# A state-space scan carried as h plus A·u: ScalarE divides u by the decay rate into PSUM, VectorE adds neighbouring tokens of two groups at once, decays in SBUF

## The chip, the core and the metric

One core of one Trainium2 chip runs the kernel. The time is device microseconds from the start to the end of one execution; the runs shown are medians of 3. The core has a matrix engine (TensorE, PE), VectorE (DVE), ScalarE (ACT), GpSimd (POOL), and a sync engine (SyncE, SP) that here only issues DMAs. Each takes its instructions strictly in order, and they meet at semaphores.

## What is computed

Four images of 3x224x224 go through a token stage (two small attention blocks over 3x3 patches, then a projection), which gives 3136 tokens of 768 channels per image. Then comes a selective state-space layer and a layer of experts. The state-space layer is what the change touches:

```
delta = softplus(x @ W_D + b_D + p_Delta)         # per token and channel
A_bar = exp(delta * A)                            # A = -1..-16, one per state n
B_bar = (A_bar - A) / (delta * A) * delta * Bproj # = (A_bar - A) / A * Bproj
h     = A_bar * h + B_bar * x                     # recurrence over tokens
y     = sum_n C_n * h_n
```

With u = B·x the input of one state is (A_bar − A)·u/A. There are 768 channels x 16 states = 12288 independent recurrences, each 3136 tokens long, per image.

## The kernel before

The program has three stages, one after the other: `performer1`, `performer2` and `tail` (line 1298). Only `tail` is touched, and it takes more than half of the time.

`tail` cuts the tokens into UNITS = 28 units (4 images x 7) of T = 448 tokens. In each unit the recurrences are done in STEPS = 24 steps, so 672 in all: step k = Q·dc + q (Q = 4) handles channel chunk dc of six (128 channels) and four of the 16 states. The 128 partitions of a step hold 32 channels x 4 states, and the free axis holds 4 groups g of 32 channels with 448 tokens each. A row of the ring `v` (RING = 6 steps deep) has 4 groups of GW = 452 columns. Step n goes through the engines like this:

- GpSimd, `weigh_in` (L1615, instruction at L1624): v = x·B, all four groups in one instruction of 128x1792. `weigh_out` (L1627, at L1636) multiplies the scanned states by C, 128x1792 again. GpSimd's order is in(k), out(k−2).
- ScalarE, `step` (L1926, at L1935): the decay exp(A·delta), one instruction per group, from `dr` in SBUF into PSUM banks 0 to 3 (`decay`, L1311), which hold one step only; so `free_pair` (L1909) makes it wait for the scan of the step before on the same pair of groups. `start_states` (L1898, at L1906) puts the last state of the unit before in front of the rows, `keep_states` (L1890, at L1896) saves the last state of a step; `weigh_out` waits for it.
- VectorE, `weigh` (L2045, at L2052): (decay − A)·v, one scalar_tensor_tensor per group; `scan` (L2054, at L2061): one tensor_tensor_scan over the 901 columns of a pair of groups. Per step that is, twice: two `weigh`, one `scan`.
- TensorE, `step` (L1725, at L1736): sums the states with `dg`, a table of diagonal matrices that carry 1/A, into bank YB; after four steps it adds h itself (L1740), and ScalarE copies the sum back into h (`add_to_h`, L1920, at L1924).

Between the steps each engine does the rest of the unit before and of the unit after. Their places are written out by hand, in the table at L1443 to L1453: a number is the step k after which an engine does the work, and on ScalarE k + 0.5 is the slot after the second pair of a step.

```
A_HW, A_SQ, A_MU, A_RS = (4, 6.5, 8, 9.5, 10.5, 12), (9.5, 12.5), 15.5, 15.5
A_MX, A_SP = (17.5, 17.5), ((18, 18.5), (19, 19.5))
V_BC, V_DL = 15, (18, 19)
A_SQ2, A_MS, A_RS2, A_EX, A_OH, A_GL = (1, 5.5), 7.5, 9.5, 12, 14, 17
V_ENC, V_IN, V_LOG, V_EQ, V_MASK = 9, (12, 14, 16, 16), 10, 11, (17, 17, 19, 19)
```

What the prediction speaks of: P_PJ is the projection of a channel chunk on TensorE (L1672, L1674) and A_HW ScalarE's copy of it into h (L1859). A_GL is four Gelu instructions (L1964) between two loads of the function table (the second from L1965). A_MX (L1880), A_SP (L1885 and L1888) and V_DL (L2042) make delta; V_BC (L2033 to L2036) makes B and C; V_IN (L2101) and V_MASK (L2127) belong to the experts; A_EX (L1956) is a small exponential for which VectorE's V_EQ waits. SyncE writes h, delta, B and C to DRAM and reads them back spread over the partitions (`spread_x`, `spread_delta`, `spread_b`, `spread_c`).

Of the kernel before, what the change touches and what calls it, by code (L numbers as in the profile page):

```python
# [21 lines left out]
T = 448  # L22
# [1256 lines left out]
RING = 6  # L1279
GW = T + 4  # L1280
AR, YB, BS, BX, BF = 4, 4, 5, 6, 7
OWN = ()
FEW = NX + 1
CAP = 30.0

def others(n):

    i, k = divmod(n, STEPS)
    return i * (STEPS - len(OWN)) + sum(j not in OWN for j in range(k + 1))  # L1290

def owned(n):

    return n + 1 - others(n)

def tail(nc, sem, w, c, t2, w1c, xd, dd, bcd, out):

    with ExitStack() as ctx:  # L1300
# [10 lines left out]
        def decay(g):  # L1311

            at = g // 2 * 1024 + g % 2 * GW
            return flat[:, at + 2:at + T + 2]

        def decays(pair):
            row = flat[:, 1024 * pair:1024 * pair + 2 * GW]
            return row.rearrange("p (g t) -> p g t", g=2)[:, :, 2:T + 2]
# [26 lines left out]
        dg = sb("dg3", [128, 4 * STEPS, 32])  # L1345
# [7 lines left out]
        mu = sb("mu", [128, 2, T])  # L1353
# [5 lines left out]
        st = sb("st3", [128, 4 * STEPS])  # L1359
        ex = sb("ex", [CH, NCH, NX])  # L1360
# [6 lines left out]
        ai, sel32, encb, wm = gm[:, 0, 0:4 * STEPS], gm[:, 1, 0:32], gm[:, 2, 0:CH], gm[:, 3, 0:6]  # L1367
# [11 lines left out]
        br, cr, zr = slice(0, N), slice(32, 32 + N), slice(32, 33 + N)  # L1379
        low, mid, top = slice(0, 32), slice(32, 64), slice(96, 128)  # L1380
# [4 lines left out]
                 (wbc[:, :, :], w["wbc"]), (pick[:, :, :], c["pick"]), (bbc[:, :], w["bbc"]), (pd[:, :], w["pd"]),  # L1385
# [9 lines left out]
        s_dgm = sem("t_diagonals_made")  # L1395
# [53 lines left out]
        P_PJ, P_SUM, P_Z = (1, 3, 4, 5, 7, 8), (9, 11), 15  # L1449
        A_HW, A_SQ, A_MU, A_RS = (4, 6.5, 8, 9.5, 10.5, 12), (9.5, 12.5), 15.5, 15.5  # L1450
        A_MX, A_SP = (17.5, 17.5), ((18, 18.5), (19, 19.5))
        V_BC, V_DL = 15, (18, 19)
        P_SUM2, P_VAR, P_IN, P_LOG, P_TURN = (2, 4), 6, (10, 11, 13, 14), 8, 10  # L1453
        P_MASK, P_OUT = (15, 15, 16, 17), (18, 19, 20, 20, 21, 22, 23, 24)
        A_SQ2, A_MS, A_RS2, A_EX, A_OH, A_GL = (1, 5.5), 7.5, 9.5, 12, 14, 17
        A_OUT = (22, 22.5, 23.5, 24, 25, 26, 27, 28)
        V_ENC, V_IN, V_LOG, V_EQ, V_MASK = 9, (12, 14, 16, 16), 10, 11, (17, 17, 19, 19)
        ROUTE, TAIL = 9, 29

        def means(i):  # L1460

            return mu[few, i % 3, :] if i % 3 < 2 else bcs[few, :]
# [16 lines left out]
        def _(sp):  # L1479
# [65 lines left out]
            def spread_c(i, q):  # L1545
                if i < UNITS:
                    for own in (True, False):
                        k = max((k for k in range(q, STEPS, Q) if (k in OWN) == own), default=None)
                        if i >= 1 and k is not None:
                            n = STEPS * (i - 1) + k  # L1550
                            sp.wait_ge(s_cv if own else s_cm, 2 * owned(n) if own else others(n))
                    spread_row(ct[:, q, :], i, 1, q).then_inc(s_lc[q], 16)
# [3 lines left out]
            sp.wait_ge(s_set, 9)  # L1556
# [14 lines left out]
            for i in range(UNITS):  # L1571
                for k in range(STEPS):
# [39 lines left out]
        def _(pool):  # L1612
            tt = nc.gpsimd.tensor_tensor

            def weigh_in(i, k):  # L1615
# [8 lines left out]
                tt(v[:, n % RING, :, 2:T + 2], xr[:, dc % 2, :].rearrange("p (i t) -> p i t", i=4), bt[:, q:q + 1, :].to_broadcast([128, 4, T]),  # L1624
                   ALU.mult).then_inc(s_v, 1)

            def weigh_out(i, k):  # L1627

                dc, q = divmod(k, Q)
                if dc == 0:  # L1630
                    pool.wait_ge(s_lc[q], 16 * (i + 1))
                if k in OWN:
                    return
                n = STEPS * i + k
                pool.wait_ge(s_st, others(n))
                tt(v[:, n % RING, :, 2:T + 2], v[:, n % RING, :, 2:T + 2], ct[:, q:q + 1, :].to_broadcast([128, 4, T]),  # L1636
                   ALU.mult).then_inc(s_cm, 1)
# [7 lines left out]
            pool.memset(v[:, :, :, T + 2:GW], 0.0).then_inc(s_set, 1)  # L1645
            pool.memset(v[:, :, :, 0:1], 0.0).then_inc(s_set, 1)
            pool.wait_ge(s_w, 16 * len(loads))
            pool.wait_ge(s_pd, 1)
            tt(dg[:, :, :], sel32[:, :].unsqueeze(1).to_broadcast([128, 4 * STEPS, 32]),
               ai[:, :].unsqueeze(2).to_broadcast([128, 4 * STEPS, 32]), ALU.mult).then_inc(s_dgm, 1)  # L1650
            for i in range(UNITS):
                for k in range(STEPS):
                    weigh_in(i, k)
                    if k >= 2:
                        weigh_out(i, k - 2)
                    elif i >= 1:
                        weigh_out(i - 1, STEPS - 2 + k)
            for k in range(STEPS - 2, STEPS):
                weigh_out(UNITS - 1, k)

        @block.tensor
        def _(pe):
# [32 lines left out]
            def front(i, k):  # L1695
                for dc in range(DC):
# [22 lines left out]
                if k == P_Z:  # L1719
# [3 lines left out]
                    mm(bank(BF), pick[mid, 0, :], bcs[mid, :], start=True, stop=True).then_inc(s_z, 1)  # L1723

            def step(i, k):  # L1725
# [5 lines left out]
                if k in OWN:  # L1731
                    pe.wait_ge(s_cv, 2 * owned(n))
                else:
                    pe.wait_ge(s_cm, others(n))
                for g in range(4):
                    last = mm(ps[32 * g:32 * g + 32, YB, 0:T], dg[:, 4 * k + g, :], v[:, n % RING, g, 2:T + 2],  # L1736
                              start=(q == 0), stop=False)
                last.then_inc(s_ns, 1)
                if q == Q - 1:
                    mm(bank(YB), ident[:, :], h[:, i % 3, dc, :], start=False, stop=True).then_inc(s_hs, 1)  # L1740

            def mlp(i, k):
# [9 lines left out]
                for m in range(MT):  # L1752
# [10 lines left out]
                    if m == 3:  # L1763
                        pe.wait_ge(s_bcs, 2 * min(i + 3, UNITS))
# [55 lines left out]
            pe.wait_ge(s_bcs, 2)  # L1820
# [4 lines left out]
            pe.wait_ge(s_dgm, 1)  # L1825
# [13 lines left out]
        def _(act):  # L1839
# [50 lines left out]
            def keep_states(i, k):  # L1890

                n = STEPS * i + k
                if k in OWN:
                    return
                act.wait_ge(s_sc, 2 * others(n))
                fn(st[:, 4 * k:4 * k + 4], v[:, n % RING, :, T + 1], ACT.Copy).then_inc(s_st, 1)  # L1896

            def start_states(i, k):  # L1898

                n = STEPS * i + k  # L1900
                if k in OWN:
                    return
                after(act, s_ns, n + 1 - RING)
                if i >= 1:
                    act.wait_ge(s_st, others(n - STEPS))
                fn(v[:, n % RING, :, 1], st[:, 4 * k:4 * k + 4], ACT.Copy,  # L1906
                   scale=0.0 if i % J3 == 0 else 1.0).then_inc(s_s0, 1)

            def free_pair(n, pair):  # L1909

                i, k = divmod(n, STEPS)
                if k in OWN:
                    act.wait_ge(s_cv, 2 * owned(n) + pair - 1)
                    at = 4 * k + 2 * pair
                    fn(st[:, at:at + 2], decays(pair)[:, :, T - 1], ACT.Copy).then_inc(s_sv, 1)
                    act.wait_ge(s_sv, 2 * owned(n) + pair - 1)
                else:
                    act.wait_ge(s_sc, 2 * others(n) + pair - 1)
# [6 lines left out]

            def step(i, k, pair):  # L1926

                dc, q = divmod(k, Q)
                n = STEPS * i + k
                if q == 0 and pair == 0:  # L1930
                    act.wait_ge(s_dr[dc % 2], 16 * ((DC // 2) * i + dc // 2 + 1))
                if n > 0:
                    free_pair(n - 1, pair)
                for g in range(2 * pair, 2 * pair + 2):
                    fn(decay(g), dr[:, dc % 2, g, :], ACT.Exp,  # L1935
                       scale=aa[:, 4 * k + g:4 * k + g + 1]).then_inc(s_a, 1)
# [56 lines left out]
            act.wait_ge(s_set, 9)  # L1993
            act.preload_act_table_set(BOTH)
            for k in range(2 * STEPS):
                front(0, k / 2)
            for i in range(UNITS + 1):
                for k in range(TAIL if i == UNITS else STEPS):
                    if i < UNITS:
                        start_states(i, k)  # L2000
                        step(i, k, 0)
# [5 lines left out]
                    if i >= 1 and k == 0:  # L2007
                        keep_states(i - 1, STEPS - 1)
                    elif i < UNITS and k > 0:
                        keep_states(i, k - 1)  # L2010
                    if i < UNITS:
                        step(i, k, 1)
# [5 lines left out]
        def _(dve):  # L2018
# [8 lines left out]
            def front(i, k):  # L2027
                if k == V_BC:
# [7 lines left out]
                    stt(bcs[br, :], ps[br, BS, 0:T], bbc[br, :], rs1[br, :], ALU.add, ALU.mult).then_inc(s_bcs, 1)  # L2036
                for half in range(2):
# [293 lines left out]
```

## Time and profile before

| | us |
|---|---|
| median of 3 runs | 8061.27 (8054.65 to 8067.14) |
| the profiled execution: its own time | 8056.0 |
| its span, first to last instruction | 8054.2 |
| busy in the span: PE, DVE, ACT, POOL | 7205.3, 6156.8, 4377.1, 5546.6 |
| mean granted TensorE clock | 0.927 of full speed |

The first two stages end at about 3200 us; the rest is `tail`. A share of busy time over the whole span mixes the stages, so the rows that matter are read within `tail`. An instruction's duration is longer than the distance between the starts of two that follow each other directly, as an engine begins the next one before the last has drained; both are used below, and told apart.

### The profile page before, as it was taken

The page shows a single profiled execution, that of the slowest core. Times are in us where ns is not written, and L with a number is a line of the kernel's source. Part 1 is how long each engine was busy: PE and PEld are TensorE (multiplying, and loading weights), DVE is VectorE, ACT ScalarE, POOL GpSimd, SP SyncE. Part 2 cuts the span into 40 slices and gives each one's busy share as a digit, 9 for nine tenths or more (in the row PEclk, how much of TensorE's full clock was granted, in tenths as well). Part 3 has the DMA queues.
Part 4 walks back from the last instruction along what each step waited for, and adds up shares of the span by engine and source line. Part 5 has one row for each costly group of instructions (what it writes and reads, how often), then busy time and mean ns, then how long its engine had stood idle before and what let it go on. Part 6 is the DMA issues. An engine that isn't in the chain of part 4 may idle for free.

```text
span 8054.2 us, 87036 instructions
## 1 busy us (share of the span) xinstructions
PE 7205.3 (89%) x31060; PEld 2876.3 (36%) x31060; DVE 6156.8 (76%) x6517; ACT 4377.1 (54%) x7837; POOL 5546.6 (69%) x2487
## 2 busy tenths in 40 slices
PE   8999999979999995689889898898888988988888
PEld 6444444323443431133333333333333333333323
DVE  2566666761333333999999999999999999999995
ACT  3566666763344442555555555555555555555553
POOL 0011111128766640999999999999999999999994
PEclk9999999989999997799899999899998999989988
DMA  1111111125545423333333333333334333334331
GB/s 40 33 46 45 42 44 43 42 60 114 105 98 109 100 61 84 101 116 113 131 130 125 112 119 125 126 124 126 119 109 136 122 128 113 117 128 132 125 110 56
DMA packets 358649, 786.32 MB, mean 98 GB/s; under 512 B 72229, under 2 KB 284727, under 8 KB 350729
## 3 DMA queue, kind: packets, MB, share of 16 engines
q1 hardware_dynamic: 320838, 689.44, 29.1%
q0 software_dynamic: 21712, 51.75, 2.5%
q10 hardware_dynamic: 15666, 39.57, 1.4%
q8 instruction: 246, 4.03, 0.2%
q14 instruction: 187, 1.52, 0.1%
HBM read 597.06 MB, written 183.35 MB: 97 GB/s over the span
## 4 chain that ended last, share of the span: by engine, by line
DVE 34%; issue 13%; ACT 7%; PE 6%; POOL 1%; DMA 0%; DVEq 0%; SPq 0%; ACTq 0%
DVE v L2052 16%; DVE v L2061 15%; ACT ps L1935 2%; PE ps L1672 2%; DVE dl L2042 1%; PE ps L1674 1%; PE ps L1667 1%; ACT dl L1880 1%; ACT gm L1964 1%; PE ps L1802 1%; PE ps L1681 1%; PE ps L1736 1%; ACT dl L1885 0%; ACT L1965 0%; ACT L1964 0%
## 5 line engine op out<-in xcount | busy, mean ns | idle before, releaser
L2061 DVE TENSOR_TENSOR_SCAN v<-ps,v 128x901 f32<-128x901 f32 x1344 | 2732.3, 2033 | 93.4 <-DVE v L2052 0.9
L1636 POOL TENSOR_TENSOR v<-v,ct 128x1792 f32<-128x1792 f32 x672 | 2258.2, 3360 | 288.8 <-ACT st L1896 285.6
L1624 POOL TENSOR_TENSOR v<-xr,bt 128x1792 f32<-128x1792 f32 x672 | 2258.2, 3361 | 65.8 <-DMA bt<-bc_rows 65.8
L1935 ACT ACTIVATE ps<-dr,aa 128x448 f32<-128x448 f32 x2688 | 1596.0, 626 | 1087.4 <-DVE v L2061 1077.7
L2052 DVE SCALAR_TENSOR_TENSOR v<-ps,aa,v 128x448 f32<-128x448 f32 x2688 | 1686.2, 669 | 11.5 <-ACT ps L1935 5.4
L236 POOL DMA_DIRECT2D tokens<-ob x448 | 235.3, 532 | 1533.5 <-DVE ob L563 1490.5
L1736 PE MATMUL ps<-v,dg 128*32 128x448 f32 x5376 | 779.3, 617 | 476.9 <-POOL v L1636 251.8
L1802 PE MATMUL ps<-w_or_w,gm 128*112 128x384 f32 x1792 | 692.4, 534 | 67.8 <-DVE gm L2127 65.0
L1896 ACT ACTIVATE st<-v 128x4 f32<-128x4 f32 x672 | 140.7, 209 | 912.5 <-DVE v L2061 910.6
L1672 PE MATMUL ps<-x,wpa 128*128 128x448 f32 x1008 | 479.0, 613 | 85.9 <-ACT h L1859 75.1
L1667 PE MATMUL ps<-h,w_or_w 128*128 128x448 f32 x1344 | 538.3, 551 | 9.7 <-DVE bcs L2036 9.7
L1802 PEld LDWEIGHTS ps<-w_or_w,gm 128*112 128x112 f32 x1792 | 331.3, 193 | 439.8 <-issue 121.6
L1674 PE MATMUL ps<-x,wpb 64*128 64x448 f32 x1008 | 450.5, 578 | 0.0
L1736 PEld LDWEIGHTS ps<-v,dg 128*32 128x32 f32 x5376 | 136.1, 113 | 856.7 <-POOL v L1636 375.1
L929 PE MATMUL ps<-xt,wa 128*64 128x448 f32 x2016 | 435.0, 565 | 0.0
L552 DVE COPY ht<-ps 112x512 f32<-112x512 f32 x112 | 77.4, 691 | 466.6 <-ACT kp L433 466.6
L1667 PEld LDWEIGHTS ps<-h,w_or_w 128*128 128x128 f32 x1344 | 251.4, 192 | 294.0 <-issue 264.5
L1238 DVE TENSOR_TENSOR kq<-ps,rsa 128x896 f32<-128x896 f32 x56 | 61.1, 1092 | 358.7 <-PE ps L937 337.5
L586 DVE RECIPROCAL qpn<-qpn 128x448 f32<-128x448 f32 x112 | 330.7, 2953 | 3.8
L1672 PEld LDWEIGHTS ps<-x,wpa 128*128 128x128 f32 x1008 | 190.9, 201 | 338.8 <-issue 230.5
L290 PE MATMUL ps<-wki,h 128*112 128x256 f32 x896 | 277.3, 391 | 1.9 <-DVE hu L544 1.9
L1674 PEld LDWEIGHTS ps<-x,wpb 64*128 64x128 f32 x1008 | 174.7, 186 | 271.0 <-issue 271.0
(331 smaller groups left out, 11534.1 us busy)
## 6 DMA issues: line engine op xcount, KB each, us to landing
xr<-h_by_channel SPq DMA_DIRECT2D x168, 896.0 KB, 5.0
dr<-delta_by_channel SPq DMA_DIRECT2D x168, 896.0 KB, 4.7
x<-tokens SPq DMA_DIRECT2D x252, 224.0 KB, 5.3
tokens<-ob POOLq DMA_DIRECT2D x448, 112.0 KB, 2.4
w_or_w<-in_w SPq DMA_DIRECT2D x29, 1536.0 KB, 6.4
w_or_w<-centred_w SPq DMA_DIRECT2D x27, 1536.0 KB, 9.1
h_by_channel<-h SPq DMA_DIRECT2D x112, 336.0 KB, 5.1
delta_by_channel<-dl SPq DMA_DIRECT2D x224, 168.0 KB, 2.8
```

Of the source, the lines that this page charges most:

```text
L586: nc.vector.reciprocal(qpn[:, u % 3, :], qpn[:, u % 3, :]).then_inc(s_dr, 1)
L929: mm(ps[half[g], o, 0:T], wa[:, j, cols], xt[:, 2 * (n % 3) + g, 0:TR2, j:j + 2 * S2 - 1:2], start=(j == 0), stop=False)
L1624: tt(v[:, n % RING, :, 2:T + 2], xr[:, dc % 2, :].rearrange("p (i t) -> p i t", i=4), bt[:, q:q + 1, :].to_broadcast([128, 4, T]), ALU.mul ...
L1636: tt(v[:, n % RING, :, 2:T + 2], v[:, n % RING, :, 2:T + 2], ct[:, q:q + 1, :].to_broadcast([128, 4, T]), ALU.mult).then_inc(s_cm, 1)
L1667: last = mm(into, weights(dc), h[:, i % 3, dc, :], start=(dc == 0), stop=(dc == DC - 1))
L1672: mm(into, even(j), x3[:, 0:TR3, j:j + 2 * S3 - 1:2], start=(j == 0), stop=False)
L1674: return mm(into, odd(j - 3), x3[0:64, 1:TR3 + 1, j - 3:j - 4 + 2 * S3:2], start=False, stop=(j == 5))
L1736: last = mm(ps[32 * g:32 * g + 32, YB, 0:T], dg[:, 4 * k + g, :], v[:, n % RING, g, 2:T + 2], start=(q == 0), stop=False)
L1802: mm(into[:, 0:D // 2], gm[:, m, cs], w2[:, m, lo:lo + D // 2], start=(m == 0), stop=False)
L1935: fn(decay(g), dr[:, dc % 2, g, :], ACT.Exp, scale=aa[:, 4 * k + g:4 * k + g + 1]).then_inc(s_a, 1)
L2052: stt(row, decay(g), aa[:, 4 * k + g:4 * k + g + 1], row, ALU.subtract, ALU.mult).then_inc(s_wt, 1)
L2061: nc.vector.tensor_tensor_scan(row, flat[:, 1024 * pair + 1:1024 * pair + GW + T + 2], row, 0.0, ALU.mult, ALU.add).then_inc(s_sc, 1)
```

## The change

Before, a row holds A·h, and one VectorE pass per group forms (decay − A)·u. Written for s = −(h + u), the recurrence is s(t) = decay(t)·(s(t−1) + u(t−1) − u(t)/A): what enters the scan is −u/A of the token plus u of its left neighbour, and the scan adds first and multiplies then. (In the units of before that state is A·h plus A·u.) Since h = −s − u, the sum over states leaves out the direct part, x times the sum of B·C over the states; it is taken off h once per unit. In the code:

- ScalarE, `divide` (new): one copy per group with the scale 1/A (negative, from `ai`), from `v` in SBUF into PSUM banks 0 to 3, 449 columns. `decays` (new): the exponentials go into a new SBUF buffer `da`, two steps deep, one step ahead of `divide`. Order of a step: start_states(n+1), divide(n, pair 0), decays(n+1, pair 0), the other work, keep_states(n−1), divide(n, pair 1), decays(n+1, pair 1), the other work.
- VectorE, `differences` (new) in place of two `weigh`: one tensor_tensor add over both groups of a pair, 128x898, in place in PSUM; `scan` reads PSUM and `da`, adds, then multiplies, over 901 columns as before. New per unit: C·B (one scalar_tensor_tensor of 16x448 in V_BC) and, at V_HK = 23, h·(1 − sum of B·C), one scalar_tensor_tensor of 128x2688.
- TensorE: `dg` is gone; the sum uses one matrix `sel32` of −1. One new matmul per unit (P_KP = 19) spreads B·C.
- GpSimd: `weigh_out` runs BEHIND = 3 steps behind `weigh_in` instead of 2; the making of `dg` is gone, two small memsets are new.
- SyncE: one more small constant is loaded; load_x moves from k = 13 to 16, the load of w2 from 15 to 16.
- The table of places is written anew.

```
-            def weigh(i, k, g):
...
-                dve.wait_ge(s_a, 4 * n + g // 2 * 2 + 2)
-                row = v[:, n % RING, g, 2:T + 2]
-                stt(row, decay(g), aa[:, 4 * k + g:4 * k + g + 1], row, ALU.subtract, ALU.mult).then_inc(s_wt, 1)
...
+            def differences(n, pair):
+
                 if pair == 0:
-                    dve.wait_ge(s_s0, others(n))
-                dve.wait_ge(s_wt, 4 * n + 2 * pair + 2)
-                nc.vector.tensor_tensor_scan(row, flat[:, 1024 * pair + 1:1024 * pair + GW + T + 2], row, 0.0, ALU.mult,
-                                             ALU.add).then_inc(s_sc, 1)
+                    dve.wait_ge(s_s0, n + 1)
+                dve.wait_ge(s_ux, 4 * n + 2 * pair + 2)
+                tt(quotients(pair), quotients(pair), v[:, n % RING, 2 * pair:2 * pair + 2, 2:T + 3],
+                   ALU.add).then_inc(s_wt, 1)
+
+            def scan(n, pair):
...
+                dve.wait_ge(s_wt, 2 * n + pair + 1)
+                dve.wait_ge(s_a, 4 * n + 2 * pair + 2)
+                nc.vector.tensor_tensor_scan(row[:, 2:GW + T + 3], flat[:, 1024 * pair + 2:1024 * pair + GW + T + 3],
+                                             a[:, 2:GW + T + 3], 0.0, ALU.add, ALU.mult).then_inc(s_sc, 1)
...
+            def decays(n, pair):
+
+                dc, q = divmod(n % STEPS, Q)
+                if q == 0:
+                    act.wait_ge(s_dr[dc % 2], 16 * ((DC // 2) * (n // STEPS) + dc // 2 + 1))
+                after(act, s_sc, 2 * n + pair - 3)
+                for g in range(2 * pair, 2 * pair + 2):
+                    at = 4 * (n % STEPS) + g
+                    fn(da[:, n % 2, g, 2:T + 2], dr[:, dc % 2, g, :], ACT.Exp, scale=aa[:, at:at + 1]).then_inc(s_a, 1)
+
+            def divide(n, pair):
+
+                act.wait_ge(s_v, n + 1)
+                after(act, s_sc, 2 * n + pair - 1)
+                for g in range(2 * pair, 2 * pair + 2):
+                    at = 4 * (n % STEPS) + g
+                    fn(quotient(g), v[:, n % RING, g, 3:T + 4], ACT.Copy, scale=ai[:, at:at + 1]).then_inc(s_ux, 1)
...
+                    dve.wait_ge(s_bcs, 2 * (i + 1))
+                    after(dve, s_kp, i)
+                    stt(cc, ps[cr, BS, 0:T], bcc[br, :], bcs[br, :], ALU.add, ALU.mult).then_inc(s_cb, 1)
+                if k == V_HK:
+                    dve.wait_ge(s_kp, i + 1)
+                    dve.wait_ge(s_xst, 64 * (i + 1))
+                    stt(h[:, i % 3, :, :], ps[:, BF:BF + 1, 0:T].to_broadcast([128, DC, T]), 1.0, h[:, i % 3, :, :],
+                        ALU.add, ALU.mult).then_inc(s_hk, 1)
...
-        P_PJ, P_SUM, P_Z = (1, 3, 4, 5, 7, 8), (9, 11), 15
-        A_HW, A_SQ, A_MU, A_RS = (4, 6.5, 8, 9.5, 10.5, 12), (9.5, 12.5), 15.5, 15.5
-        A_MX, A_SP = (17.5, 17.5), ((18, 18.5), (19, 19.5))
-        V_BC, V_DL = 15, (18, 19)
-        P_SUM2, P_VAR, P_IN, P_LOG, P_TURN = (2, 4), 6, (10, 11, 13, 14), 8, 10
-        P_MASK, P_OUT = (15, 15, 16, 17), (18, 19, 20, 20, 21, 22, 23, 24)
-        A_SQ2, A_MS, A_RS2, A_EX, A_OH, A_GL = (1, 5.5), 7.5, 9.5, 12, 14, 17
-        A_OUT = (22, 22.5, 23.5, 24, 25, 26, 27, 28)
-        V_ENC, V_IN, V_LOG, V_EQ, V_MASK = 9, (12, 14, 16, 16), 10, 11, (17, 17, 19, 19)
+        P_PJ, P_SUM, P_Z = (0, 3, 5, 6, 7, 8), (8, 11), 15
+        A_HW, A_SQ, A_MU, A_RS = (4, 7.5, 8, 9.5, 10.5, 11.5), (9.5, 12.5), 16, 15.5
+        A_MX, A_SP = (17.5, 18.5), ((18, 18.5), (18.5, 18.5))
+        V_BC, V_DL = 15, (18, 18)
+        P_KP, V_HK = 19, 23
+        P_SUM2, P_VAR, P_IN, P_LOG, P_TURN = (2, 4), 6, (9, 11, 13, 13), 8, 9
+        P_MASK, P_OUT = (15, 15, 16, 16), (17, 18, 19, 20, 21, 22, 23, 24)
+        A_SQ2, A_MS, A_RS2, A_EX, A_OH, A_GL = (0, 5.5), 7.5, 8.5, 12, 14.5, 17
+        A_OUT = (21, 22, 23, 23.5, 24.5, 25.5, 26.5, 27.5)
+        V_ENC, V_IN, V_LOG, V_EQ, V_MASK = 8, (12, 14, 16, 16), 10, 11, (17, 17, 18, 18)
```

## Rows read from the trace of the kernel before

**Rows 1.** The profile page, part 1: busy time, share and instructions of each engine.

```profile
PE 7205.3 (89%) x31060; PEld 2876.3 (36%) x31060; DVE 6156.8 (76%) x6517; ACT 4377.1 (54%) x7837; POOL 5546.6 (69%) x2487
```

**Rows 2.** Busy time of each engine in one stretch of the last stage, granted clock, DMA.

```profile
5000.00:5500.00 500.00, 442.69 (x1630) 162.56 (x1628) 488.42 (x505) 283.70 (x596) 470.99 (x142) 0.91 0.38 125
```

**Rows 3.** VectorE in order of time, five pieces of undisturbed steps: start, us, instruction.

```profile
5075.51 2.03 DVE L2061 TENSOR_TENSOR_SCAN v<-ps,v 128x901 f32<-128x901 f32 x1
5077.46 1.25 DVE L2052 SCALAR_TENSOR_TENSOR v<-ps,aa,v 128x448 f32<-128x448 f32 x2
5078.74 2.03 DVE L2061 TENSOR_TENSOR_SCAN v<-ps,v 128x901 f32<-128x901 f32 x1
5080.69 1.25 DVE L2052 SCALAR_TENSOR_TENSOR v<-ps,aa,v 128x448 f32<-128x448 f32 x2
5082.05 2.03 DVE L2061 TENSOR_TENSOR_SCAN v<-ps,v 128x901 f32<-128x901 f32 x1
```

**Rows 4.** GpSimd: the line of `weigh_in` over the whole trace, and two neighbours in time.

```profile
L1624 POOL TENSOR_TENSOR v<-xr,bt x672: 3347/3359/3392, 3198.6 to 7935.4; 128x1792 f32<-128x1792 f32 x168
...
5061.56 3.36 POOL L1636 TENSOR_TENSOR v<-v,ct 128x1792 f32<-128x1792 f32 x1
5064.88 3.36 POOL L1624 TENSOR_TENSOR v<-xr,bt 128x1792 f32<-128x1792 f32 x1
```

**Rows 5.** Groups by line and shape, VectorE, whole trace: busy us, mean ns, idle before.

```profile
L2061 DVE TENSOR_TENSOR_SCAN v<-ps,v 128x901 f32<-128x901 f32 x1344 | 2732.3, 2033 | 93.4 <-DVE v L2052 0.9 <-ACT v L1906 0.5
L558 DVE TENSOR_TENSOR gl<-ps,rs 128x896 f32<-128x896 f32 x112 | 121.2, 1082 | 6.0 <-PE ps L265 6.0
L1238 DVE TENSOR_TENSOR kq<-ps,rsa 128x896 f32<-128x896 f32 x56 | 61.1, 1092 | 358.7 <-PE ps L937 337.5 <-issue 21.2
L2042 DVE SCALAR_TENSOR_TENSOR dl<-ps,pd,dl 128x448 f32<-128x448 f32 x168 | 103.6, 671 | 8.1 <-ACT dl L1888 8.1
L2143 DVE TENSOR_TENSOR wpa<-wpa,wma 128x2304 f32<-128x2304 f32 x1 | 2.6, 2559 | 0.0
```

**Rows 6.** Groups by line and shape, ScalarE, whole trace.

```profile
L1935 ACT ACTIVATE ps<-dr,aa 128x448 f32<-128x448 f32 x2688 | 1596.0, 626 | 1087.4 <-DVE v L2061 1077.7 <-DMA dr<-delta_by_channel 9.3
L1924 ACT ACTIVATE h<-ps 128x448 f32<-128x448 f32 x168 | 89.1, 530 | 5.3 <-PE ps L1740 5.3
L1964 ACT ACTIVATE gm<-gm,b 128x448 f32<-128x448 f32 x112 | 68.9, 660 | 11.4 <-DVE gm L2101 10.5
```

**Rows 7.** ScalarE in order of time around its steps 17 to 19 of one unit.

```profile
5018.13 1.20 ACT L1935 ACTIVATE ps<-dr,aa 128x448 f32<-128x448 f32 x2 [3.83 <-DVE v L2061]
5019.34 1.28 ACT L1964 ACT_TABLE_LOAD   x1
5020.63 2.47 ACT L1964 ACTIVATE gm<-gm,b 128x448 f32<-128x448 f32 x4
5023.12 1.28 ACT L1965 ACT_TABLE_LOAD   x1
...
5024.53 1.18 ACT L1935 ACTIVATE ps<-dr,aa 128x448 f32<-128x448 f32 x2
5025.73 3.26 ACT L1880 ACTIVATE dl<-ps,pc 128x448 f32<-128x448 f32 x6
...
5030.48 1.45 ACT L1885 ACTIVATE dl<-dl,small 128x1344 f32<-128x1344 f32 x1
...
5033.01 1.34 ACT L1888 ACTIVATE dl<-dl 128x1344 f32<-128x1344 f32 x1
```

**Rows 8.** VectorE in order of time, the experts' work within the same steps.

```profile
5021.24 1.13 DVE L2101 TENSOR_TENSOR gm<-ps,rs2t 128x448 f32<-128x448 f32 x2
...
5029.01 1.12 DVE L2127 TENSOR_TENSOR gm<-gm,ps 128x448 f32<-128x448 f32 x2
```

**Rows 9.** Who waited for whom on ScalarE, 4000 to 7500 us: total us, times, longest.

```profile
ACT ps L1935 <- DVE v L2061: 789.7, 403, 4.7
ACT h L1859 <- PE ps L1674: 34.4, 25, 3.2
```

More of the change, by code:

```diff
@@ L1279 @@
 RING = 6
+BEHIND = 3
 GW = T + 4
 AR, YB, BS, BX, BF = 4, 4, 5, 6, 7
-OWN = ()
 FEW = NX + 1
 CAP = 30.0
[L1287 to L1295, printed above, removed]
 def tail(nc, sem, w, c, t2, w1c, xd, dd, bcd, out):
@@ L1309, in tail, with quotient, quotients @@
         flat = ps[:, :, :].rearrange("p k n -> p (k n)")
-        def decay(g):
+        def quotient(g):
             at = g // 2 * 1024 + g % 2 * GW
-            return flat[:, at + 2:at + T + 2]
-        def decays(pair):
+            return flat[:, at + 2:at + T + 3]
+        def quotients(pair):
             row = flat[:, 1024 * pair:1024 * pair + 2 * GW]
-            return row.rearrange("p (g t) -> p g t", g=2)[:, :, 2:T + 2]
+            return row.rearrange("p (g t) -> p g t", g=2)[:, :, 2:T + 3]
         ident = sb("ident3", [128, 128])
@@ L1546, in spread_c @@
                 if i < UNITS:
[L1547 to L1551, printed above, removed]
+                    after(sp, s_cm, STEPS * (i - 1) + STEPS - Q + q + 1)
                     spread_row(ct[:, q, :], i, 1, q).then_inc(s_lc[q], 16)
@@ L1819, in _ @@
             pe.wait_ge(s_wv, 16)
[L1820 removed]
+            pe.wait_ge(s_cb, 1)
             pe.wait_ge(s_mu, 1)
@@ L1924, in add_to_h @@
                 fn(h[:, i % 3, dc, :], bank(YB), ACT.Copy).then_inc(s_hy, 1)
[L1926 to L1936, printed above, removed]
             def mlp(i, k):
@@ L1996, in _ @@
                 front(0, k / 2)
+            start_states(0)
+            for pair in range(2):
+                decays(0, pair)
             for i in range(UNITS + 1):
                 for k in range(TAIL if i == UNITS else STEPS):
+                    n = STEPS * i + k
+                    if n + 1 < STEPS * UNITS:
+                        start_states(n + 1)
                     if i < UNITS:
-                        start_states(i, k)
-                        step(i, k, 0)
+                        divide(n, 0)
+                    if n + 1 < STEPS * UNITS:
+                        decays(n + 1, 0)
                     if i >= 1 and k == 2:
@@ L2006, in _ @@
                     others_due(i, k)
[L2007 to L2010, printed above, removed]
+                    if 0 < n <= STEPS * UNITS:
+                        keep_states(n - 1)
                     if i < UNITS:
-                        step(i, k, 1)
+                        divide(n, 1)
+                    if n + 1 < STEPS * UNITS:
+                        decays(n + 1, 1)
                     others_due(i, k + 0.5)
@@ L2081, in step @@
             def step(i, k):
                 for pair in range(2):
-                    weigh(i, k, 2 * pair)
-                    weigh(i, k, 2 * pair + 1)
-                    if k in OWN:
-                        own_scan(i, k, pair)
-                    else:
-                        scan(i, k, pair)
+                    differences(STEPS * i + k, pair)
+                    scan(STEPS * i + k, pair)
             def mlp(i, k):
```

144 lines of the change are left out of this document (58 added, 86 removed).

## The prediction

> **What bounds the kernel now.** I read the page's busy shares first, then the windows inside the last stage, then each engine in order of time. Over the whole span TensorE looks busiest [rows 1], but that mixes three stages. In a window of the last stage VectorE is busy 488 of 500 us, GpSimd 471, TensorE 443, ScalarE 284 [rows 2]. In order of time VectorE shows no gap [rows 3], while ScalarE waits 790 us for VectorE's scans in 3500 [rows 9]: VectorE sets the pace.
>
> The sizes: `weigh_in` starts at 3198.6 for step 0 and at 7935.4 for step 671 [rows 4], so a step takes 7.06 us and a unit of 24 steps 169.4. Undisturbed, two pairs of VectorE's take 82.05 − 75.51 = 6.54 us [rows 3], 157.0 a unit; the other 12.4 us are its work for the experts, delta, B and C. GpSimd starts an instruction every 3.32 us [rows 4], 6.64 a step, 159.2 a unit. That is the next floor: whatever VectorE saves, no more than 169.4 − 159.2 = 10.2 us a unit, 286 us in 28 units, can be had.
>
> **VectorE: the difference.** A pair is now: scan, and 1.95 us after its start the first of two `weigh`; from that start to the next scan 1.28 or 1.36 us, as the last one has to land and a semaphore be passed (0.03 us behind the landing with one wait, 0.11 with two) [rows 3]. Mean 3.27. After: one add of 128x898. Two rows have its size and kind, 1082 and 1092 ns for 896 columns [rows 5]; I take 1.085. Its output lies in PSUM, which neither row shows; the ends are 1.08 and, if it cost no less than the two instructions it replaces, 1.25. Both scans now pass two semaphores (differences, decays), so 0.11 twice. 1.95 + 1.085 + 0.11 = 3.145: saved 0.125 x 1344 = **168 us**.
>
> The scan keeps its 901 columns and one PSUM and one SBUF input, but adds before it multiplies. No row shows that form. I take the 2033 ns of [rows 5]; upward nothing in the trace bounds it better than a few per cent (5% would be 137 us), downward one operation in the loop instead of two would halve it, and then GpSimd's floor is met. 
>
> **VectorE: what is added.** h·(1 − sum) over 2688 columns: between 896 and 2304 columns a VectorE column costs (2559 − 1092)/1408 = 1.04 ns [rows 5], so 2.96 us, less about 0.08 of overlap: 2.9. C·B: as the 671 ns row [rows 5] with its wait, 0.7. Together 3.6 x 28 = **101 us**, all of it on the engine that sets the pace. VectorE alone thus gains only 67 us.
>
> **ScalarE: is it still cover?** It now issues eight big instructions a step instead of four. Nearest to the scaled copy are the exponential with a scale from memory, 626 ns, and the plain copy from PSUM, 530 [rows 6]; a pair of the former lasts 1.18, so starts lie 0.56 apart [rows 7]. I take 0.56 for all four of a half step, plus 0.11 for the small state copy: 2.35 of 3.145 us. Today it is 1.23 of 3.27. Its other work is 284/500 x 169.4 = 96 us a unit less 48 x 1.23 = 37 us; new total 48 x 2.35 + 37 = 150 us of some 166. On average it fits; the question is bursts. PSUM still holds one step, so a quotient can't be made ahead: from the end of the scan that frees it, 0.03 + 0.11 + 0.56 + 0.62 = 1.3 us go by until the pair is ready, and VectorE wants it after 3.06. The reserve is 1.75 us, and each half step has only 0.8 us for other work. Decays a step ahead do not widen it, since they stand in the same queue behind the divide.
>
> At k = 17 stand the Gelus with both table loads, 5019.34 to 5024.40 = 5.06 us [rows 7]. Let T be the end of the first scan of step 16. ScalarE: half step to T + 2.35, Gelus to 7.4, quotients of (17, pair 1) ready at 8.7. VectorE, with its two V_IN products of 1.13 [rows 8], wants them at 3.06 + 1.13 + 3.145 = 7.3: stall 1.4. Next, three A_MX (half of 3.26) end at 11.4; VectorE finds (18, 0) ready. h copy and exponential, 0.5 + 1.4, put (18, 1) at 16.95; VectorE, with two V_MASK of 1.12 [rows 8], wants it at 16.1: stall 0.85. The slot 18.5 holds 1.65 + 1.34 + 1.4 + 1.34 = 5.7 us [rows 7] and ends at 23.7; VectorE needs the last logarithm for delta at 23.0: stall 0.7. Sum 2.95 x 27 = **80 us**; ends 0 and 5 us a unit.
>
> Elsewhere ScalarE waits for TensorE's projections, 34.4 us in 20.7 units, at most 3.2 [rows 9], today inside its idle time. In the new table A_HW's last copy (11.5) stands ahead of A_EX (12), for which VectorE waits. Of the 1.7 us a unit I let 0.6 through: **16 us**, ends 0 and 47.
>
> The Trainium skill (ScalarE: Activation LUTs, in the part on the pipeline for one element) prefers PSUM to SBUF as ScalarE's target and so speaks against moving the decays. Here the scaled exponential into PSUM has 626 ns and the Gelu within SBUF 660 [rows 6], which agrees in sign; at 0.034 us more for two instructions the burst stalls would be about 0.3 us a unit longer, 8 us in all.
>
> **What costs nothing.** GpSimd one step further behind: it waits for the state copies, so the in-order product behind it is late, but its 10 us of idle time a unit cover that; without the cover each late product delays TensorE's sum by 3.3 us and `add_to_h` after it. The making of `dg` at the start: GpSimd waits there for B's transfer anyway. TensorE's new matmul, one of about 0.6 us a unit: 443 of 500 busy leaves 19 us a unit. SyncE's loads moved to k = 16: h and weights are used from k = 0 and 17 on, 8 and more steps or the masks' wait later; a weight load late would show as TensorE waiting for a DMA. `dr` is wanted one step (6.6 us) earlier, but is also released one step earlier, and at a unit's turn there remain four steps. At the start the first step waits for four exponentials and two copies instead of two exponentials: **3 us**.
>
> **Sum.** −168 + 101 + 80 + 16 + 3 = +32 us on the profiled execution's 8056.0: 8088. The median of the runs shown is 5 us above it, so 8093 for a median. A measurement tells about 0.2%, 16 us, from no change.
>
> **Rivals.** *ScalarE keeps up* (faster). The two late stalls vanish if the real copies are nearer the plain 530 ns, and work VectorE does meanwhile fills the rest: 8061 − 67 + 3 = 7997, down to 7950 if the semaphore costs 0.03 throughout (−47). For it: 790 us of ScalarE idle [rows 9]. Against: the Gelu block is three times the reserve, and its position is written in the table. It decides where the quotients of step 17, pair 1, come within 7.3 us of T.
>
> *ScalarE becomes the bound.* If scaled copies and exponentials into SBUF come 0.60 apart like the Gelus ((2.47 − 0.66)/3, [rows 7]), a half step has 0.6 us left, each wait for TensorE's projections falls on VectorE whole (1.7 us), the burst stalls grow to about 4.5 and the bursts at 7.5 to 9.5 stall for another 1.5: 7.7 us a unit, 8061 − 67 + 3 + 215 = 8212. For it: 2.35 of 3.145 us are gone before any other work; against it: the averages still leave 10%.
>
> *The replacement doesn't do what it says.* If the add over PSUM takes 1.25 us, a pair lasts 3.31 instead of 3.27 and nothing is saved: 8061 + 54 + 101 + 3 = 8219 before any stall. If the scan were cheaper by half, GpSimd sets the pace at 159.2 a unit: 8061 − 286 = 7775, little changed by anything else.
>
> **Chances.** Forecast (the gain given back by stalls and the new products) 0.47, its own range 8035 to 8140; ScalarE keeps up 0.32; ScalarE the bound 0.16; dearer add or scan 0.03; cheaper scan 0.02. Faster by over 0.2% takes the second case, the last and a little of the first; no change the first's lower part. The range 7960 to 8220 leaves out some 2 in 10.
>
> **What would show it.** VectorE's adds near 1085 ns, 1344 of them, and the scans still at 2033; a pair 3.1 to 3.2 us apart in undisturbed steps; VectorE idle before the add, waiting for ScalarE's copies, 50 to 150 us in all and most of it around the Gelus; ScalarE busy near 90% in the last stage; the product over 2688 columns near 2.96 us. I am wrong if VectorE shows no such waits (then it is faster), if they are spread over all steps (then ScalarE is the bound), or if GpSimd is seen without idle time.

## The result, and the profile after

The changed kernel takes 7980.58 us (median of 4 runs, 7977.03 to 7982.75) against 8062.83 for the kernel before on the same chips: ratio 0.9898, 95% interval 0.9886 to 0.9911. It is 1.0% faster; the forecast was 8093 us, slower by 0.4%. The profiled execution took 7978.7 us, its span is 7977.0, 77.2 us shorter than before. The first step of the last stage starts where it did, so all of it was won in the 672 steps.

Part 1 of the page, as in [rows 1]:

```profile
PE 7204.1 (90%) x31116; PEld 2913.0 (37%) x31116; DVE 6031.6 (76%) x5230; ACT 5851.7 (73%) x10525; POOL 5539.2 (69%) x2488
```

and the window of 5000 to 5500 us, with the columns of [rows 2] (us; busy and count of PE, its weight loads, DVE, ACT, POOL; clock; DMA share; GB/s):

```profile
5000.00:5500.00 500.00, 448.36 (x1668) 170.27 (x1668) 483.23 (x375) 445.00 (x893) 477.62 (x145) 0.94 0.38 124
```

ScalarE went from 284 to 445 of 500 us, 89%, as forecast. VectorE fell from 488 to 483 and GpSimd rose from 471 to 478: no engine is full any more, and four engines lie within 38 us of each other. The groups by line, as in [rows 5] and [rows 6]:

```profile
L2051 DVE TENSOR_TENSOR_SCAN v<-ps,da 128x901 f32<-128x901 f32 x1344 | 2732.5, 2033 | 46.1
L2042 DVE TENSOR_TENSOR ps<-ps,v 128x898 f32<-128x898 f32 x1344 | 1452.3, 1081 | 74.2 <-ACT ps L1907 70.7
L1907 ACT ACTIVATE ps<-v,ai 128x449 f32<-128x449 f32 x2688 | 1593.6, 625 | 222.9 <-DVE v L2051 216.4
L1899 ACT ACTIVATE da<-dr,aa 128x448 f32<-128x448 f32 x2688 | 1634.0, 656 | 9.5 <-DMA dr<-delta_by_channel 9.5
```

The scan kept its 2033 ns, the add costs 1081, the scaled copy 625 and the exponential into SBUF 656 instead of 626 into PSUM: durations as they were priced. What was not priced right is a distance. VectorE in order of time (compare [rows 3]):

```profile
5071.94 2.03 DVE L2051 TENSOR_TENSOR_SCAN v<-ps,da 128x901 f32<-128x901 f32 x1
5073.89 1.07 DVE L2042 TENSOR_TENSOR ps<-ps,v 128x898 f32<-128x898 f32 x1
5075.00 2.03 DVE L2051 TENSOR_TENSOR_SCAN v<-ps,da 128x901 f32<-128x901 f32 x1
5076.95 1.07 DVE L2042 TENSOR_TENSOR ps<-ps,v 128x898 f32<-128x898 f32 x1
5078.06 2.04 DVE L2051 TENSOR_TENSOR_SCAN v<-ps,da 128x901 f32<-128x901 f32 x1
```

A pair takes 3.06 us, not 3.145: behind the end of the add the scan starts after 0.03 us, in both pairs, though it waits for two semaphores. Before, the mean pair took 3.27. That is 0.21 x 1344 = 282 us saved in place of 168.

The burst (the stretch of k = 17 to 18.5 with the Gelus, the two table loads and the work for delta on ScalarE) went as worked out. ScalarE from the half step (17, pair 0) to the last logarithm of delta, with the lines that bound it, and VectorE's three waits in it:

```profile
4990.72 1.20 ACT L1907 ACTIVATE ps<-v,ai 128x449 f32<-128x449 f32 x2 [1.41 <-DVE v L2051]
...
4993.09 1.28 ACT L1941 ACT_TABLE_LOAD   x1
4994.38 2.35 ACT L1941 ACTIVATE gm<-gm,b 128x448 f32<-128x448 f32 x4
4996.75 1.28 ACT L1942 ACT_TABLE_LOAD   x1
...
5012.71 1.32 ACT L1874 ACTIVATE dl<-dl 128x1344 f32<-128x1344 f32 x1
```

```profile
4999.37 1.10 DVE L2042 TENSOR_TENSOR ps<-ps,v 128x898 f32<-128x898 f32 x1 [1.56 <-ACT ps L1907]
...
5007.47 1.10 DVE L2042 TENSOR_TENSOR ps<-ps,v 128x898 f32<-128x898 f32 x1 [0.81 <-ACT ps L1907]
...
5014.13 1.87 DVE L2034 SCALAR_TENSOR_TENSOR dl<-ps,pd,dl 128x448 f32<-128x448 f32 x3 [0.68 <-ACT dl L1874]
```

ScalarE is busy without a gap from 4990.7 to 5014.0, 23.3 us (23.7 forecast), and VectorE waits 1.56, 0.81 and 0.68 (1.4, 0.85 and 0.7 forecast). In the waits of 4000 to 7500 us, 21 units, that pattern is nearly all there is on VectorE, and GpSimd waits in the same place only:

```profile
DVE ps L2042 <- ACT ps L1907: 52.2, 44, 1.8
DVE dl L2034 <- ACT dl L1874: 14.3, 21, 0.7
DVE gm L2070 <- PE ps L1652: 8.8, 20, 0.5
```

```profile
POOL v L1625 <- ACT st L1880: 156.8, 63, 4.0
```

63 waits in 21 units are three a unit, 7.5 us. GpSimd in order of time shows them around one burst, and none between it and the next:

```profile
4998.33 3.36 POOL L1625 TENSOR_TENSOR v<-v,ct 128x1792 f32<-128x1792 f32 x1 [2.57 <-ACT st L1880]
...
5006.43 3.36 POOL L1625 TENSOR_TENSOR v<-v,ct 128x1792 f32<-128x1792 f32 x1 [1.42 <-ACT st L1880]
...
5016.54 3.36 POOL L1625 TENSOR_TENSOR v<-v,ct 128x1792 f32<-128x1792 f32 x1 [3.43 <-ACT st L1880]
```

`weigh_in` runs from 3198.5 to 7858.2, 166.7 us a unit instead of 169.4. GpSimd's 159.2 of work plus 7.5 of waits give that number, but so does the work plus the waits of any engine, so the sum does not say which one sets the pace. Part 4 of the page follows back from the last instruction what released what; this chain lay mostly on VectorE before (first line, shares of the whole span) and is spread over four engines now (second line), TensorE first:

```profile
DVE 34%; issue 13%; ACT 7%; PE 6%; POOL 1%; DMA 0%; DVEq 0%; SPq 0%; ACTq 0%
PE 18%; ACT 12%; DVE 12%; issue 12%; POOL 7%; ACTq 0%; DMA 0%; DVEq 0%; POOLq 0%
```

In the unit of the rows above it goes over VectorE, with short pieces on ScalarE, from the end of the burst at 5014 to 5056, over ScalarE to 5062, over TensorE (its part of the experts, projections, sums) to 5100 and, after 9 us on ScalarE, from 5109 to 5132, over VectorE to 5158 and over ScalarE's next burst. What each of them is worth had to be tried.

### The profile page after: what moved, and what is told of

Same layout as the page of the kernel before. It is cut to its first block, busy times and chain, and to the rows that moved or that the text cites. A ratio compares the mean times of both kernels' runs of the same rounds, so it can differ in the third digit from the quotient of the medians.

```text
span 7977.0 us, 90814 instructions
## 1 busy us (share of the span) xinstructions
PE 7204.1 (90%) x31116; PEld 2913.0 (37%) x31116; DVE 6031.6 (76%) x5230; ACT 5851.7 (73%) x10525; POOL 5539.2 (69%) x2488
## 4 chain that ended last, share of the span: by engine, by line
PE 18%; ACT 12%; DVE 12%; issue 12%; POOL 7%; ACTq 0%; DMA 0%; DVEq 0%; POOLq 0%
DVE ps L2042 6%; POOL v L1625 4%; PE ps L1657 4%; PE ps L1659 4%; ACT da L1899 4%; DVE v L2051 4%; ACT ps L1907 3%; POOL v L1615 3%; PE ps L1722 2%; PE ps L1652 2%; PE ps L1789 1%; PE ps L1675 1%; PE ps L1676 1%; ACT dl L1866 1%; ACT dl L1871 1%
## 5 line engine op out<-in xcount | busy, mean ns | idle before, releaser
L2051 DVE TENSOR_TENSOR_SCAN v<-ps,da 128x901 f32<-128x901 f32 x1344 | 2732.5, 2033 | 46.1
L1625 POOL TENSOR_TENSOR v<-v,ct 128x1792 f32<-128x1792 f32 x672 | 2269.5, 3377 | 216.7 <-ACT st L1880 216.7
L1907 ACT ACTIVATE ps<-v,ai 128x449 f32<-128x449 f32 x2688 | 1593.6, 625 | 222.9 <-DVE v L2051 216.4
L1899 ACT ACTIVATE da<-dr,aa 128x448 f32<-128x448 f32 x2688 | 1634.0, 656 | 9.5 <-DMA dr<-delta_by_channel 9.5
L2042 DVE TENSOR_TENSOR ps<-ps,v 128x898 f32<-128x898 f32 x1344 | 1452.3, 1081 | 74.2 <-ACT ps L1907 70.7
L1722 PE MATMUL ps<-v,sel 128*32 128x448 f32 x5376 | 773.3, 609 | 544.2 <-ACT h L1913 304.5
L1789 PE MATMUL ps<-w_or_w,gm 128*112 128x384 f32 x1792 | 725.7, 554 | 4.4 <-DMA w_or_w<-in_w 2.2
L1789 PEld LDWEIGHTS ps<-w_or_w,gm 128*112 128x112 f32 x1792 | 348.0, 203 | 429.6 <-issue 193.2
L1722 PEld LDWEIGHTS ps<-v,sel 128*32 128x32 f32 x5376 | 154.9, 112 | 894.8 <-POOL v L1625 371.1
L1657 PE MATMUL ps<-x,wpa 128*128 128x448 f32 x1008 | 450.7, 582 | 20.0 <-DVE enc L2126 11.1
L1129 ACT ACTIVATE kqs<-kq,bkq 128x448 f32<-128x448 f32 x112 | 68.8, 661 | 279.8 <-DVE kq L1238 279.8
```

The lines of the kernel that those rows point to most:

```text
L1657: mm(into, even(j), x3[:, 0:TR3, j:j + 2 * S3 - 1:2], start=(j == 0), stop=False)
L1722: last = mm(ps[32 * g:32 * g + 32, YB, 0:T], sel32[:, :], v[:, n % RING, g, 2:T + 2], start=(q == 0), stop=False)
L1789: mm(into[:, 0:D // 2], gm[:, m, cs], w2[:, m, lo:lo + D // 2], start=(m == 0), stop=False)
L1899: fn(da[:, n % 2, g, 2:T + 2], dr[:, dc % 2, g, :], ACT.Exp, scale=aa[:, at:at + 1]).then_inc(s_a, 1)
L1907: fn(quotient(g), v[:, n % RING, g, 3:T + 4], ACT.Copy, scale=ai[:, at:at + 1]).then_inc(s_ux, 1)
L2042: tt(quotients(pair), quotients(pair), v[:, n % RING, 2 * pair:2 * pair + 2, 2:T + 3], ALU.add).then_inc(s_wt, 1)
```

## The experiments

Medians against the kernel before on the same chip, of 8059.7 to 8061.4 us. A difference to the changed kernel is taken from its 7980.6, measured at another time; the kernels before measured beside each run agree within 3.2 us.

**1. Which wait costs 0.08 us.** In the kernel before, only the scan of pair 0 has a wait for the first states in front of it.

```
                 if g == 0:
                     dve.wait_ge(s_v, n + 1)
+                    dve.wait_ge(s_s0, others(n))
...
-                if pair == 0:
-                    dve.wait_ge(s_s0, others(n))
                 dve.wait_ge(s_wt, 4 * n + 2 * pair + 2)
```

> Kernel before, with VectorE's wait for the first states moved from in front of the scan of pair 0 to in front of its first weigh. In the kernel before, the scan of pair 0 starts 0.11 us behind the last weigh, that of pair 1 (no such wait) 0.03. Theory 1 (a wait standing between the last product and the scan costs 0.08 us though its semaphore was set long ago): the gap falls to 0.03 for both pairs, 672 x 0.08 = 54 us, time near 8007. Rival (the gap belongs to pair 0 for another reason, such as the banks or ScalarE's writes): gap stays at 0.11, time within 16 us of 8061.

8018.2 us, ratio 0.9949 (0.9937 to 0.9962): 42 us less from moving one wait. Both pairs are now 3.23 to 3.24 us apart:

```profile
5073.82 2.03 DVE L2060 TENSOR_TENSOR_SCAN v<-ps,v 128x901 f32<-128x901 f32 x1
5075.77 1.25 DVE L2053 SCALAR_TENSOR_TENSOR v<-ps,aa,v 128x448 f32<-128x448 f32 x2
5077.06 2.03 DVE L2060 TENSOR_TENSOR_SCAN v<-ps,v 128x901 f32<-128x901 f32 x1
```

Theory 1 holds. Of the 54 us expected 42 came: over all scans the idle time before them fell by 47 us (93.4 to 46.2), and in the 3500 us window VectorE's waits for TensorE and ScalarE grew a little (2.0 to 6.8 and 0.5 to 4.1). A time equal to half of what the change won could be had in the old kernel by moving this line.

**2. The same, the other way round,** in the changed kernel:

```
-                dve.wait_ge(s_wt, 2 * n + pair + 1)
+                dve.wait_ge(s_s0, n + 1)
                 dve.wait_ge(s_a, 4 * n + 2 * pair + 2)
+                dve.wait_ge(s_wt, 2 * n + pair + 1)
```

> Changed kernel, with the scan's waits written in another order and one more ahead of them: first states, decays, then the differences last. Theory 1 in its strong form (each wait passed ahead of the one that really blocks costs 0.08 us): the scan starts 0.11 or 0.19 us behind the add instead of 0.03, plus 108 to 215 us on 7980. Rival (waits whose semaphores are set are passed while the add still runs and cost nothing): gap 0.03, 7980 within 16 us.

8073.6 us, 93 more. The scan now starts 0.13 us behind the add (5077.51 against 5076.30 + 1.08), the pair takes 3.16:

```profile
5074.35 2.03 DVE L2052 TENSOR_TENSOR_SCAN v<-ps,da 128x901 f32<-128x901 f32 x1
5076.30 1.08 DVE L2042 TENSOR_TENSOR ps<-ps,v 128x898 f32<-128x898 f32 x1
5077.51 2.03 DVE L2052 TENSOR_TENSOR_SCAN v<-ps,da 128x901 f32<-128x901 f32 x1
```

So it is not the number of waits alone. With the blocking wait first and a set one behind it (the changed kernel) the gap is 0.03; with one set wait ahead (the scan of pair 0 in the kernel before) 0.11; with two 0.13. Over all scans the idle time before them says the same: 180.0/1344 = 0.13 here, 46.1/1344 = 0.03 in the changed kernel. The rival is out: waits that are long fulfilled are not passed for free under the running instruction when the blocking one comes last. The change had put the blocking wait first, and my count of semaphores could not see that.

This run is also the nearest to the kernel that the forecast priced: with the gap at 0.13 instead of the forecast's 0.11, the changed kernel is 0.2% slower than the kernel before (ratio 1.0019, 1.0010 to 1.0027). The wider gap adds 134 us of idle time and costs 93, as VectorE's waits for ScalarE shrink (52.2 to 41.7 us in 3500). The order was not reversed without the extra wait, so 0.11 for one set wait ahead rests on the kernel before.

**3. One add or two.**

```
+                for g in range(2 * pair, 2 * pair + 2):
...
+                    tt(quotient(g), quotient(g), v[:, n % RING, g, 2:T + 3], ALU.add).then_inc(s_wt, 1)
```

> Changed kernel, with the add done per group again (two of 128x449 in place of one of 128x898). Two adds start 0.52 us apart and the second lasts 0.605, so a pair takes 1.95 + 0.52 + 0.605 + 0.03 = 3.11 us instead of 3.06: plus 0.05 x 1344 = 60 us, near 8040. This says how much of the gain is the joining of two groups, and how much the plainer instruction (add instead of subtract and multiply, 0.67 us). Rival (the joining is what brings the gain): near 8130.

8036.1 us, 55 more, the two adds 1.14 us instead of 1.08. Joining the groups is worth 55 us; the rest of VectorE's gain belongs to the plainer instruction and the order of the waits, which this run does not tell apart.

**4. Does VectorE set the pace?** The product over 2688 columns at k = 23, 2931 ns by its row, cut to 8 columns, so that h keeps the direct part; runs 5 and 6 leave it out too.

> Changed kernel without the product over 128x2688 that takes the direct part off h (an instruction of 8 columns stands in its place, so the direct part is left out of the result). If VectorE still sets the pace, its 2.93 us per unit come off whole: minus 28 x 2.8 = 78 us, near 7902. If GpSimd or ScalarE has become the bound, the time falls by less than 30 us, to 7950 or more.

7977.8 us: no change. The forecast's term for it was 81 us. VectorE's time went into new waits for ScalarE, 105.2 us instead of 52.2 in 21 units. The new ones do not stand at the burst but at step 8, where ScalarE itself waits 1.91 us for TensorE's sums and 1.86 for its projection. VectorE in order of time, only the lines with idle time ahead, of one such place:

```profile
5098.19 1.10 DVE L2041 TENSOR_TENSOR ps<-ps,v 128x898 f32<-128x898 f32 x1 [1.31 <-ACT ps L1907]
...
5102.95 1.10 DVE L2041 TENSOR_TENSOR ps<-ps,v 128x898 f32<-128x898 f32 x1 [1.59 <-ACT ps L1907]
```

GpSimd's waits stayed the three of the burst (154.7 us for 63). The chain of the page moved from VectorE to GpSimd, at the same time:

```profile
POOL 18%; PE 16%; issue 11%; ACT 10%; DVE 6%; DMA 0%; ACTq 0%; DVEq 0%; POOLq 0%
```

In one unit it goes over GpSimd alone from 5017.8 to 5074.3 and over TensorE from there to 5101, where the changed kernel's went over VectorE and TensorE: behind the burst two queues of nearly equal length run side by side, and shortening one leaves the other. The next two runs put an instruction of nearly the same length (2809 ns) back, here at k = 12, in the other run at k = 23.

```
+                if k == 12:
+                    nc.vector.reduce_sum(spare[:, :], ident[:, :].unsqueeze(1).to_broadcast([128, 20, 128]),
+                                         mybir.AxisListType.X)
```

**5. At k = 23.**

> The kernel without the direct part's product (which came out as fast as the changed one) with another VectorE instruction of 2.8 us per unit in its place at k = 23 (a sum over 128x2560 of a constant, its result unused; the direct part is left out of the result). Theory A (from k = 19 to 17 of the next unit GpSimd runs without a gap and sets the pace; VectorE has room behind the burst up to about k = 8, where ScalarE waits for TensorE anyway): 7978 within 16 us. Theory C (the missing product changed nothing because the profile of it was wrong, or VectorE is nowhere the bound): the same; the pair with the next run tells them apart.

7978.6 us: free.

**6. At k = 12.**

> The same instruction of 2.8 us, at k = 12 instead of 23, with the direct part's product left out. Theory A: VectorE runs without a gap from k = 9 to the burst at 17, so each microsecond there makes the burst start later and GpSimd wait longer: plus 2.8 x 27 = 75 us, near 8050. Theory C (VectorE has 2.8 us a unit to spare wherever): 7978.

8044.7 us: 66 more for the same instruction (28 times, 79 us of work), and GpSimd's waits rise from 154.7 to 208.3 us, still 63 of them. Theory C is out. Theory A holds for the stretch before the burst: there VectorE's work delays the burst, and with it the state copies that GpSimd waits for. It does not hold that GpSimd sets the pace from the burst to the next one: in this run's trace the chain of a unit goes over GpSimd from 5042 to 5099 only, then over TensorE to 5126, ScalarE to 5135, TensorE to 5158 and VectorE to 5174. All three runs lack the product; whether the changed kernel itself would take more VectorE work at k = 23 for free was not tried, and no run made GpSimd's or TensorE's work longer or shorter.

**7. The burst made shorter.** If that is so, moving two pairs of decays out of it must pay in full.

```
+            def next_decays(n, pair):
+                half = 2 * (n % STEPS) + pair
+                for _ in range(0 if half in (34, 35) else 2 if half in (41, 45) else 1):
...
+                        decays(made[0] // 2, made[0] % 2)
```

> Changed kernel with another order on ScalarE alone: at k = 17 the two pairs of decays are left for later (two halves of a step then run without lead) and made up at k = 20 and 22. 2 x 1.12 us of ScalarE's queue leave the stretch between the Gelus and the last logarithm of delta. Theory A (the period of a unit is set where ScalarE's burst at k = 17 to 18.5 holds up VectorE, and behind it GpSimd, which waits for the state copies only there): 2.1 to 2.2 us less per unit, minus 57 us, near 7923, and GpSimd's waits fall from 7.4 to about 5.2 us a unit. Theory B (GpSimd and TensorE set the pace and the burst is covered): no change, 7965 to 7995.

7929.3 us (7924.1 to 7932.4), ratio to the kernel before 0.9837 (0.9824 to 0.9851): 51 us less than the changed kernel (57 expected) by an order of ScalarE's queue alone. VectorE's waits for copies fell from 52.2 to 18.0 us and GpSimd's to 118.9. This is the fastest version found. The waits of the same 3500 us:

```profile
POOL v L1625 <- ACT st L1880: 118.9, 64, 3.5
...
DVE ps L2051 <- ACT ps L1907: 18.0, 30, 1.2
```

**8. The decays ahead of the divide,** everywhere.

> Changed kernel with the decays of the next step ahead of the divide in each half of a step. Each quotient is 1.12 us later after the scan that frees it, so VectorE's reserve falls from 1.7 to 0.6 us, while ScalarE's total is the same. My stall count as predicted: the three stalls of the burst grow by up to 1.1 each and most slots with 1.5 us of other work stall too, 3 to 6 us a unit, 8060 to 8150. Rival (only ScalarE's chain through the burst counts, the reserve does not): below 8000.

8011.0 us, 30 more, below the expected range and above the rival's. VectorE's waits for ScalarE rose from 52.2 to 93.7 us, 103 times instead of 44, by 2 us a unit instead of 3 to 6, since those about delta vanished. The reserve counts, at half the weight I gave it.

**9. GpSimd two steps behind, not three.**

> Changed kernel with the product with C two steps behind the product with B, as before the change, instead of three. GpSimd's room between the two shrinks by one step, so it must wait sooner when VectorE falls behind: if that room is what carries VectorE's late steps, its waits at k = 17 to 23 grow and the time rises by 50 us or more, to 8030 or above. If the room was not needed (the forecast's view, one step costs nothing), within 16 us of 7980.

7992.6 us, 12 more, which is not clear of no change at the 16 us that a measurement tells. The view that the room between the products carries the burst, 50 us or more, is out; the third step is worth little.

**10. The old table of places.**

> Changed kernel with the places of the kernel before (the two new ones kept, 19 and 23). Both delta logarithms then stand at 18.5 and 19.5 and VectorE's sums of delta at 18 and 19, the masks at 19. Theory A: the burst is spread over one more half step, other waits for TensorE come back; within 40 us of 7980 on either side. If the new table is what makes the change pay: above 8030.

8022.0 us, 41 more, between the two expectations (up to 8020, above 8030): half of the change's gain hangs on the new places. Waits for copies are 82.5 us (66 times), and VectorE waits for TensorE 27.8 instead of 8.8.

**11 and 12. Two more edits of the table,** on top of the late decays.

> The kernel with late decays, and the projections of chunks 1 and 2 on TensorE at k = 1 and 4 instead of 3 and 5. In the late-decays kernel ScalarE waits 1.5 and 1.9 us at k = 4 and 8 for projections, and VectorE 1.2 behind it near k = 8. Theory A: that wait shrinks by about 1 us a unit, minus 15 to 30 us on 7929. If TensorE only follows GpSimd's products there: within 16 us of 7929.

7970.9 us, 42 more than without it: a miss. ScalarE now waits for TensorE's second sums, with its squares in line behind them:

```profile
ACT sq L1836 <- PE ps L1677: 59.0, 57, 1.4
ACT h L1845 <- PE ps L1659: 39.6, 59, 1.6
```

The squares at 5.5 now follow the sums one by one, 1.2 us of waiting each, three times, and VectorE's next add comes 3.1 us late.

> The kernel of the run before, with delta's pieces spread: A_MX at 17.5 and 18, A_SP at 18.5 and 19.5, V_DL at 18 and 19, P_KP at 20. 2.7 us of ScalarE's queue move behind the burst, VectorE's second sum of delta one step later: GpSimd's longest wait (3.4 us at k = 18 to 19) shrinks, minus 1 to 1.5 us a unit, 25 to 40 us below the run before. If the total lag of VectorE counts and not its place: no change.

7984.6 us, 14 more again. Spreading delta's pieces did not help; GpSimd waits 151 times instead of 89 for the same total (152.6 and 150.9), as the second expectation had it. Why it is 14 us slower was not found, and whether the spreading would help without the moved projections was not tried.

## Why the prediction was wrong

- **What failed** is one term of the step "VectorE: the difference": "Both scans now pass two semaphores (differences, decays), so 0.11 twice." It was 0.03 twice. The saving was 282 us, not 168; those 114 us are the whole distance from the +32 us of the sum to the −77 measured, give or take 5. Rows 3 showed 0.11 and 0.03, and I read them as two waits against one; runs 1 and 2 show that what counts is whether a fulfilled wait stands ahead of the blocking one. That the sum closes so well is in part luck: run 2 shows that a wider gap costs about 0.7 of its size, and run 4 that the 82 us of the product cost nothing.
- The add: 1.085 us taken, 1.081 measured. The scan in add-then-multiply form: 2033 ns as taken. The Trainium skill (DVE: opcode table, instruction layouts, handler registers and perf-mode slots, section 6) says that the scan runs at half throughput because its result is routed back to an earlier stage; that the two orders cost the same was my reading of it, and the trace agrees with that (2033 ns in both). The product over 2688 columns: 2.96 taken, 2.93 measured.
- ScalarE: 2.35 us a half step and three stalls of 2.95 us in sum; measured 2.33 (5013.94 to 5016.27) and 3.05. Exponentials into SBUF cost 0.030 us more than into PSUM in duration (0.034 taken). The Trainium skill (ScalarE: Activation LUTs, Step-by-step: what each stage is for) calls PSUM the lower-latency target, and the trace agrees in sign; the distance between starts is 1.12 us for two exponentials into SBUF and for two copies into PSUM alike, so nothing was lost in the queue. The small term for A_EX did not come: VectorE shows no wait there; in run 9 it does (17.9 us).
- "ScalarE keeps up" was the rival of the right sign, at 7997 down to 7950 with the semaphore at 0.03; but its mechanism, no stalls, is not what happened. The stalls came in full, and without the semaphore's part the sign would not have turned (run 2). Its last term was also summed wrongly: 0.03 throughout is 0.08 x 1344 = 108 us, not 47, so that rival reaches down to 7889, and with the forecast's 96 us of waits it gives 7985.
- "VectorE sets the pace" was right of the kernel before and not of the changed one. VectorE's work and waits add up to the period (−282 + 101 + 100 of waits + 3 = −78), as they must, but run 4 took 82 us of its work away for nothing, since GpSimd's queue is nearly as long there. The stretch where VectorE's work was shown to count is from k = 12 to the burst. My windows of 500 us averaged over it.
- The floor was set too low: 159.2 us a unit for GpSimd leaves out the 7.5 us that it waits around the burst for ScalarE's state copies, which stand in line behind the Gelus and the work for delta. With them it is 166.7, what was measured, and only shortening the burst (run 7) brought it down.
- The range, 7960 to 8220, held the time; the sign did not.

## What to carry to other kernels

Put the wait that really blocks first, and those that are fulfilled long before behind it: on VectorE one such wait taken out of the way gained 42 us in one kernel, and the reverse order with one more wait cost 93 in the other. Where four engines are within some per cent of each other, ask in which part of the period each one's work counts, by the chain of the page and by adding the same instruction in two places; then take work out of the burst in the one queue that bounds it, even if it runs with less lead there. Edits of a hand-written schedule that look free in one view (runs 11 and 12) have to be tried one by one.

## What the runs showed of the hardware that I had not expected

- On VectorE, from the end of an instruction to the start of the next that waits for it: 0.03 us if that wait comes first (changed kernel) or alone (run 1), 0.11 with one fulfilled wait ahead (kernel before), 0.13 with two (run 2).
- GpSimd's instruction of 128x1792 lasts 3377 ns instead of 3360 with ScalarE at 89%, 3.40 in some stretches, while the distance between starts stays at 3.32 us: it cost nothing.
- Filling ScalarE from 57% to 89% of the window of 5000 to 5500 us left VectorE's scan at 2033 ns and its smaller products within 1% (L2034: 677 ns, 671 before).
